# Retention stage written out step by step: side work laid out anew, q's row scale moved into the clip bounds, four buffers of absolute values

## The chip, the core and the metric

The kernel runs on one core of a Trainium2 chip. TensorE (PE) multiplies matrices and writes PSUM, VectorE (DVE) and ScalarE (ACT) work elementwise and read both PSUM and SBUF, GpSimd (POOL) works elementwise on SBUF, and SyncE (SP) issues the DMAs. Each engine takes its own instructions in order; semaphores order the engines among each other. The metric is the device time of one execution in microseconds (us): 2624.17 before, the median of 3 runs (2622.93 to 2625.43).

## The reference, cut to what matters

Eight batches of 1024 tokens (32x32) with 256 channels go through three parts one after the other: a retention layer (with a group norm ahead of it and a residual behind it), a causal attention layer, and a dense mixture of eight experts. The change touches the computation of the first part alone. For every batch and each of 8 heads of 32 channels:

```
q = xf @ Wq.T ; k = xf @ Wk.T * SCALING ; vr = xf @ Wv.T        # xf: group-normed x
qr = theta_shift(q, sin, cos) ; kr = theta_shift(k, sin, cos)   # x * cos + rotate_every_two(x) * sin
qk = einsum('bhqd,bhkd->bhqk', qr, kr) * mask                   # mask[h,i,j] = gamma**dist / sqrt(row sum)
den = clip(abs(qk).sum(-1, keepdims=True), 1.0, 50000.0)
out = einsum('bhqk,bhkd->bhqd', qk / den, vr)                   # then layer norm per head, gelu, @ Wo.T
```

The row sum of the mask factors into a part of the query's row of the image, a part of its column, and head. The kernel applies the decay and the column's part as a window that is multiplied onto the scores; the row's part is one factor for each query row and head.

## The kernel before, in words

The retention layer is `layer0`. A batch has 4 phases p (two groups g of 4 heads, by two halves c of 512 queries), and a phase has 8 steps kt, one for each 128 keys; B = 8 batches make 32 phases and 256 steps. In a step, PE writes the scores of the *next* step for 4 heads (`scores`, L325, two halves j of two heads), then the sums of absolute values of the step before (`sums`, L350, into the PSUM bank `den`), then the weighted values of this step (`weighted`, L339, into `num`). DVE multiplies the scores by the window (`products`, L488, 128x1024, twice a step), and ACT takes their absolute value (`absolutes`, L679, twice a step) into one of four buffers, that is two steps' worth; so it waits until `sums` has read the one of two steps ago (`den_done`, i - 1).

Around these steps lies side work, which each engine has in its own order, by hand, at fixed steps kt. It comes through two more PSUM banks, pA and pB, each a queue of tasks in a fixed order (`A_MID`, `B_MID`); a task on PE first waits (`a_free`, `b_free`) until its predecessor in the bank has been read out.

- Preparation of the next q and k tile: `project` (L264) into pA; the tile is read into t1, for q by DVE with the row scale (`q_rotate_in`, L464), for k by ACT (`k_take`, L659); then `shuffle` (DVE L472), `rotate_cos` (POOL L766), `rotate_sin` (DVE L477), the sum (`split`, POOL L772), a rounded copy (`high`, ACT L666), the remainder (`low`, POOL L779), and 12 DMAs by SP that stack both into qst or kst (L161). t1, t2, hi and lo are single, so the preparations go one behind the other.
- v: `project_v` (L273), read out by ACT (`v_take`, L670).
- The end of a phase, done in the next one (tag 3' is the last phase of the batch before): ACT takes num and den (L683, L687), PE turns them (`transpose_n` L285 into pB, `transpose_d` L291 into pA), DVE takes head sums, centres, clips den (L496, L501, L510), ACT squares (L692), DVE sums (`variance`, L515), POOL works out and applies the factor (`scale_heads`, L794 to L804, with a power at L801), PE turns back (`transpose_z`, L297), ACT applies gelu (L696), and `out_proj` (L307) and `add_residual` (L557) end it.
- Group norm of the next batch: `statistics`, `aggregate` on DVE, two small matmuls `gn1` and `gn2` into pA (L280), `group_mean`, `group_var`, POOL's `group_rstd` (L789), `normalise` (L551). Here gn1 and gn2 stand at kt 2 and 3 of phase 2, and the k projection of that phase at kt 5 and 6.

Batches 0 and 7 are written out; batches 1 to 6 are one body in a hardware loop on each engine (`Fori`), so there are 5 jumps back. The attention part (`layer1_attention`) and the experts (`layer1_experts`) have the same form: first batch, a loop over 6, last batch.

## Time and profile before

| what | value |
|---|---|
| median of 3 runs | 2624.17 us |
| the profiled execution's own time | 2624.51 us |
| its span in the trace | 2622.4 us |
| granted TensorE clock, mean | 0.984 |
| busy: PE, DVE, ACT, POOL | 96%, 70%, 55%, 20% |
| retention up to 1122 us, attention from there to about 1517, experts to the end | |

The busy shares are means over three parts that differ. TensorE works in all of them; what the others' shares mean depends on what TensorE waits for, and that is read from its own rows. Around the span lie 2.1 us that the time of the run has and the trace hasn't.

### The profile page before, as it was taken

Reading aid. Unit: us, or ns where it says so; the run is one execution under the profiler, and the core shown is the slowest. Engines: PE = TensorE matmul, PEld = TensorE weight load, DVE = VectorE, ACT = ScalarE, POOL = GpSimd, SP = SyncE. Lnnn points to the kernel's source line nnn. Section 1 sums busy time; section 2 is a strip of 40 time slices with the busy share of each in tenths; the row PEclk is TensorE's granted clock in tenths of the full one; section 3 lists DMA queues with packets and bytes.
Section 4 is the critical chain, followed back from the end, with each engine's and each line's share of the span. In section 5 each row is a group of like instructions: output and inputs, shape, how many; then the busy total and the mean of one; then the engine's idle time right before and its main releaser. Section 6 shows DMA issues by size and latency. Waiting matters only on the chain. (4 is left out here: it accounts for less than half of the span.)

```text
span 2622.4 us, 43895 instructions
## 1 busy us (share of the span) xinstructions
PE 2512.7 (96%) x15328; PEld 1786.7 (68%) x15328; DVE 1834.2 (70%) x2847; ACT 1449.9 (55%) x2044; POOL 517.6 (20%) x444
## 2 busy tenths in 40 slices
PE   5999999999999999979999969999999999999999
PEld 2444444444444444369999958888888888888888
DVE  4878777777777777657777757666666666666665
ACT  2666565566566566636566545555555555555554
POOL 2333333333333333201212110000000000000000
PEclk8999999999999999989999979999999999999999
DMA  6232222222232222123223143000000000000000
GB/s 233 51 85 60 77 62 79 65 72 75 56 85 59 83 59 70 49 71 111 82 77 115 49 146 106 18 24 24 18 23 24 24 24 24 24 24 24 24 17 16
DMA packets 116786, 157.95 MB, mean 60 GB/s; under 512 B 16272, under 2 KB 82328, under 8 KB 116384
## 3 DMA queue, kind: packets, MB, share of 16 engines
q1 hardware_dynamic: 116640, 156.01, 20.1%
q8 instruction: 91, 1.49, 0.3%
q14 instruction: 55, 0.45, 0.1%
HBM read 72.03 MB, written 33.59 MB: 40 GB/s over the span
## 5 line engine op out<-in xcount | busy, mean ns | idle before, releaser
L488 DVE TENSOR_TENSOR l_prod<-l_scores,l_window 128x1024 f32<-128x1024 f32 x512 | 615.6, 1218 | 220.7 <-PE l_scores L325 186.0
L679 ACT ACTIVATE l_absp<-l_prod 128x1024 f32<-128x1024 f32 x512 | 521.9, 1053 | 282.8 <-PE l_den L350 233.6
L1696 ACT ACTIVATE e_r<-e_h,e_bn,e_rs 128x512 f32<-128x512 f32 x512 | 399.4, 781 | 485.7 <-PE e_h L1547 484.5
L325 PE MATMUL l_scores<-l_qst,l_kst 96*128 96x512 f32 x1024 | 369.3, 457 | 27.9 <-DMA l_qst<-l_lo 12.0
L325 PEld LDWEIGHTS l_scores<-l_qst,l_kst 96*128 96x128 f32 x1024 | 167.4, 190 | 288.3 <-issue 147.9
L1547 PE MATMUL e_y<-e_whi,e_h2lo 128*128 128x256 f32 x1024 | 289.8, 283 | 0.0
L1546 PE MATMUL e_y<-e_wlo,e_h2hi 128*128 128x256 f32 x1024 | 289.7, 283 | 0.0
L1545 PE MATMUL e_y<-e_whi,e_h2hi 128*128 128x256 f32 x1024 | 289.2, 282 | 0.1
L350 PE MATMUL l_den<-l_absp,l_ones 128*32 128x512 f32 x2048 | 274.7, 609 | 0.0
L339 PE MATMUL l_num<-l_prod,l_v 128*32 128x512 f32 x2048 | 269.3, 598 | 0.0
L1791 DVE CAST e_h1hi<-e_r 128x512 fp32r<-128x512 f32 x256 | 111.2, 434 | 224.3 <-ACT e_r L1696 220.2
L1862 POOL TENSOR_TENSOR e_res<-e_res,e_bias 128x1024 f32<-128x1024 f32 x16 | 41.4, 2590 | 930.8 <-DMA e_res<-t_scratch 930.8
L1807 DVE TENSOR_TENSOR e_h2lo<-e_r,e_h2hi 128x512 fp32r<-128x512 f32 x256 | 202.3, 804 | 8.3
L1545 PE MATMUL e_h<-e_xhi,e_whi 128*128 128x512 f32 x512 | 203.0, 397 | 5.0 <-DVE e_wlo L1735 5.0
L1546 PE MATMUL e_h<-e_xlo,e_whi 128*128 128x512 f32 x512 | 202.7, 396 | 0.0
L1547 PE MATMUL e_h<-e_xhi,e_wlo 128*128 128x512 f32 x512 | 200.9, 392 | 0.0
L1545 PEld LDWEIGHTS e_y<-e_whi,e_h2hi 128*128 128x128 f32 x1024 | 196.0, 191 | 5.3 <-DVE e_h2lo L1807 0.3
L1546 PEld LDWEIGHTS e_y<-e_wlo,e_h2hi 128*128 128x128 f32 x1024 | 196.0, 191 | 5.0
L1546 PE MATMUL e_h<-e_h1lo,e_whi 128*128 128x512 f32 x512 | 199.2, 389 | 0.0
L1545 PE MATMUL e_h<-e_h1hi,e_whi 128*128 128x512 f32 x512 | 199.2, 389 | 0.0
L1547 PE MATMUL e_h<-e_h1hi,e_wlo 128*128 128x512 f32 x512 | 199.2, 389 | 0.0
L1547 PEld LDWEIGHTS e_y<-e_whi,e_h2lo 128*128 128x128 f32 x1024 | 196.1, 191 | 0.0
(191 smaller groups left out, 4472.2 us busy)
## 6 DMA issues: line engine op xcount, KB each, us to landing
l_kst<-l_hi SPq DMA_DIRECT2D x256, 64.0 KB, 2.0
l_qst<-l_hi SPq DMA_DIRECT2D x256, 64.0 KB, 2.0
l_raw<-in_xT SPq DMA_DIRECT2D x8, 1024.0 KB, 5.6
l_kst<-l_lo SPq DMA_DIRECT2D x128, 64.0 KB, 2.0
l_qst<-l_lo SPq DMA_DIRECT2D x128, 64.0 KB, 2.0
l_xo<-in_x SPq DMA_DIRECT2D x32, 256.0 KB, 2.8
x_scratch<-l_xo SPq DMA_DIRECT2D x32, 256.0 KB, 2.3
l_xr<-x_scratch SPq DMA_DIRECT2D x8, 1024.0 KB, 8.0
```

The source lines that it names most:

```text
L325: mm = nc.tensor.matmul(sc[j][:, s, :], kst[g][0:96, h, 128 * kt:128 * kt + 128], qst[c][0:96, h, :], start=True, stop=True)
L339: mm = nc.tensor.matmul(num[32 * h:32 * h + 32, :], vsb[g][:, kt, 32 * h:32 * h + 32], prod[2 * (i % 2) + h // 2][:, h % 2, :], start=(kt ...
L350: mm = nc.tensor.matmul(den[32 * h:32 * h + 32, :], ones[:], absp[2 * (i % 2) + h // 2][:, h % 2, :], start=(kt == 0), stop=(kt == KT - 1))
L488: nc.vector.tensor_tensor(prod[n % 4][:], sc[j][:], win[:, 4 * g + 2 * j:4 * g + 2 * j + 2, w0:w0 + QC], ALU.mult).then_inc(prod_ready, 1)
L679: nc.scalar.activation(absp[n % 4][:], prod[n % 4][:], ACT.Abs).then_inc(abs_ready, 1)
L1545: nc.tensor.matmul(o, a[0], b[0], start=start, stop=False, skip_group_check=True)
L1546: nc.tensor.matmul(o, a[0], b[1], start=False, stop=False, skip_group_check=True)
L1547: return nc.tensor.matmul(o, a[1], b[0], start=False, stop=stop, skip_group_check=True)
L1696: nc.scalar.activation(r[m][:], p[m][:], ACT.Relu, bias=bn_[layer][1][:, m, e:e + 1], scale=rs[layer][:, m, e:e + 1]).then_inc(done, 1)
L1791: nc.vector.tensor_copy(h1hi[u % 2][:, m, :], r1[m][:]).then_inc(hi1_ready, 1)
L1807: nc.vector.tensor_tensor(h2lo[u % 2][:, m, :], r2[m][:], h2hi[u % 2][:, m, :].bitcast(F32), ALU.subtract).then_inc(lo2_ready, 1)
L1862: nc.gpsimd.tensor_tensor(flat(res[c][:]), flat(res[c][:]), flat(bias[c][:]), ALU.add).then_inc(biased[c], 1)
```

## The change

In `layer0` the loops over batches go: one Python loop over 256 steps S (phase P = S // 8, kt = S % 8) writes out all instructions of every engine. The side work gets new steps, the same in each phase: on PE q's projection at kt 0, transpose_n at 1, k's projection at 2, transpose_d at 3, output projection at 4 (a second one at 5 where p = 2), v's projection at 6, transpose_z at 7; gn1 and gn2 move from phase 2 to kt 4 and 5 of phase 1, and `normalise` to kt 1 of phase 2. DVE, ACT and POOL are laid out to go with it. The output projection of a batch's first half (o0), which stood at kt 7 of its phase 3, now stands in phase 0 of the next batch, and for the last batch behind the steps.

ACT reads q's projection as it reads k's (`take`), without the row scale; den is clipped against two tables instead of two constants (`clip_den`, two small DVE operations): 1/scale and 50000/scale for each query and head, which gives the same quotient. The absolute values have four steps' worth of buffers (eight tiles of 128x1024, ABS = 4), so ACT waits for the sums of four steps ago. The host makes the tables, and the program reserves less SBUF for DMA scratch. In the attention and expert parts, each `Fori` becomes a Python loop; nothing else changes there.

```diff
-    STEPS, PHASES = 4 * KT, 4
+    PHASES = 4 * B
+    ABS = 4
...
+    def outs(P):
+
+        b = P // 4 - 1
+        if b < 0:
+            return []
+        return {0: [(b, 0, 0)], 1: [(b, 0, 1)], 2: [(b, 1, 0), (b, 1, 1)], 3: []}[P % 4]
...
+    a_tasks = ["gn1", "gn2", "k", "v", "q", "v'", "k'"]
+    b_tasks = []
+    for P in range(PHASES):
+        a_tasks += [("q", P)] if has_q(P) else []
+        a_tasks += [("k", P)] if has_kv(P) else []
+        a_tasks += [("dT", P - 1)] if P else []
+        a_tasks += [("gn1", P), ("gn2", P)] if has_gn(P) else []
+        a_tasks += [("v", P)] if has_kv(P) else []
+        b_tasks += [("nT", P - 1)] if P else []
+        b_tasks += [("o", *o) for o in outs(P)]
+        b_tasks += [("zT", P - 1)] if P else []
+    a_tasks += [("dT", PHASES - 1)]
+    b_tasks += [("nT", PHASES - 1), ("o", B - 1, 0, 0), ("o", B - 1, 0, 1), ("zT", PHASES - 1), ("o", B - 1, 1, 0),
+                ("o", B - 1, 1, 1)]
+    a_order = {t: n for n, t in enumerate(a_tasks)}
+    b_order = {t: n for n, t in enumerate(b_tasks)}
+    o_order = {t[1:]: n for n, t in enumerate(t for t in b_tasks if t[0] == "o")}
...
-        rsc = sb("rowscale", [128, 2, ROWS])
+        bounds = sb("clip", [128, 2, 4, 16])
...
-        absp = [sb(f"absp{n}", [128, 2, QC]) for n in range(4)]
+        absp = [[sb(f"absp{s}_{j}", [128, 2, QC]) for j in range(2)] for s in range(ABS)]
...
-                        if part == 1 and kt == 1 and post:
-                            A("dT" + tag, transpose_d, ph)
-                        if part == 1 and p == 2 and kt == 2 and not last:
-                            A("gn1", group_sums, mv[:, :, 0], agg_done, b + 2)
...
-                        if p != 2 and kt == 3 and prep_kv:
-                            A(f"k{p}", project, wk, (1 - p // 2), p % 2, part)
-                        if p == 2 and kt == 5 + (1 - part) and prep_kv:
-                            pe.wait_ge(xn_ready, 2 * b + 3 + (1 - part))
-                            A(f"k{p}", project, wk, (1 - p // 2), p % 2, 1 - part)
...
-                        if kt == 7 and p == 3:
-                            Bk("o0", out_proj, 0, 0, 4 * b + 3, part)
...
-            body(0, True, False)
-            with pe.Fori(1, B - 1) as b:
...
+            def side_tasks(P, kt, part):
+
+                b, p = P // 4, P % 4
+                G, half = P // 2 + 1, P % 2
+                if kt == 0 and has_q(P):
+                    if part == 0:
+                        a_free(("q", P))
+                    project(wq, (P + 1) // 2 % 2, (P + 1) % 2, (part,))
+                if kt == 1 and part == 0 and P > 0:
+                    transpose_n(P - 1)
+                if kt == 2 and has_kv(P):
+                    if part == 0:
+                        a_free(("k", P))
+                        pe.wait_ge(xn_ready, 2 * (G // 2) + 2)
+                    project(wk, G % 2, half, (part,))
+                if kt == 3 and part == 1 and P > 0:
+                    transpose_d(P - 1)
+                if kt == 4 and part == 1 and has_gn(P):
+                    a_free(("gn1", P))
+                    group_sums(mv[:, :, 0], agg_done, b + 2)
+                if kt == 4 and outs(P):
+                    out_proj(*outs(P)[0], (part,))
+                if kt == 5 and part == 0 and has_gn(P):
+                    a_free(("gn2", P))
+                    group_sums(gvar[:], gvar_ready, b + 2)
+                if kt == 5 and len(outs(P)) == 2:
+                    out_proj(*outs(P)[1], (part,))
+                if kt == 6 and has_kv(P):
+                    if part == 0:
+                        a_free(("v", P))
+                    project_v(G % 2, half, (part,))
+                if kt == 7 and part == 0 and P > 0:
+                    transpose_z(P - 1)
+
+            for S in range(KT * PHASES):
+                for part in range(2):
+                    if S + 1 < KT * PHASES:
+                        scores(S + 1, part)
+                    side_tasks(S // KT, S % KT, part)
+                if S > 0:
+                    sums(S - 1)
+                weighted(S)
+            sums(KT * PHASES - 1)
+            last = PHASES - 1
+            transpose_n(last)
+            transpose_d(last)
+            out_proj(B - 1, 0, 0, (0, 1))
+            out_proj(B - 1, 0, 1, (0, 1))
+            transpose_z(last)
+            out_proj(B - 1, 1, 0, (0, 1))
+            out_proj(B - 1, 1, 1, (0, 1))
...
-            def q_rotate_in(n, a, g, c):
-
-                if not isinstance(n, int) or n > 0:
-                    dve.wait_ge(lo_ready, n)
-                dve.wait_ge(a_ready, a + 1)
-                nc.vector.tensor_tensor(t1[:].rearrange("p (a b) -> p a b", b=32), pA[:].rearrange("p (a b) -> p a b", b=32),
-                                        rsc[:, g, CROWS * c:CROWS * c + CROWS].unsqueeze(2).to_broadcast([128, CROWS, 32]),
-                                        ALU.mult).then_inc(t1_ready, 1)
...
+            def clip_den(P):
+
+                dve.wait_ge(a_ready, a_order["dT", P] + 1)
+                nc.vector.tensor_tensor(dent[:], nT_A[:, :, 0], bounds[:, 0, P % 4, :], ALU.max).then_inc(den_floor, 1)
+                dve.wait_ge(den_floor, P + 1)
+                nc.vector.tensor_tensor(dent[:], dent[:], bounds[:, 1, P % 4, :], ALU.min).then_inc(den_ready, 1)
...
+            for S in range(KT * PHASES):
+                P, kt = S // KT, S % KT
+                b, p = P // 4, P % 4
+                stats_next = b + 1 < B
+                if S == 2 * KT:
+                    dve.wait_ge(window_in, 16)
+                products(S, 0)
+                if kt == 2 and has_q(P):
+                    rotate_sin(prep_q(P), (P + 1) % 2)
+                if kt == 3 and P > 0:
+                    centre(P - 1)
+                if kt == 4 and has_kv(P):
+                    rotate_sin(prep_k(P), P % 2)
+                products(S, 1)
+                if kt == 0 and p == 1 and stats_next:
+                    statistics(b + 1, (2,))
+                if kt == 1 and has_q(P):
+                    shuffle(prep_q(P))
+                if kt == 1 and p == 1 and stats_next:
+                    statistics(b + 1, (3,))
+                if kt == 1 and p == 2 and stats_next:
+                    normalise(b + 1)
+                if kt == 2 and P > 0:
+                    head_sums(P - 1)
+                if kt == 2 and p == 1 and stats_next:
+                    aggregate(b + 1)
+                if kt == 3 and has_kv(P):
+                    shuffle(prep_k(P))
+                if kt == 4 and P > 0:
+                    clip_den(P - 1)
+                if kt == 5 and has_gn(P):
+                    group_mean(b + 1, a_order["gn1", P])
+                if kt == 5 and len(outs(P)) == 2:
+                    add_residual(*outs(P)[0])
+                if kt == 5 and P > 0:
+                    variance(P - 1)
+                if kt == 6 and has_gn(P):
+                    group_var(b + 1, a_order["gn2", P])
+                if kt == 6 and outs(P):
+                    add_residual(*outs(P)[-1])
+                if kt == 7 and p == 0 and stats_next:
+                    statistics(b + 1, (0, 1))
+            last = PHASES - 1
+            head_sums(last)
+            centre(last)
+            clip_den(last)
+            add_residual(B - 1, 0, 0)
+            variance(last)
+            add_residual(B - 1, 0, 1)
+            add_residual(B - 1, 1, 0)
+            add_residual(B - 1, 1, 1)
...
-            def absolutes(b, i, first):
-                for j in range(2):
-                    n = 2 * i + j
-                    act.wait_ge(prod_ready, 2 * STEPS * b + n + 1)
-                    if not (first and i < 2):
-                        act.wait_ge(den_done, STEPS * b + i - 1)
-                    nc.scalar.activation(absp[n % 4][:], prod[n % 4][:], ACT.Abs).then_inc(abs_ready, 1)
...
+            def take(n, a, scale):
+                nc.scalar.activation(t1[:], pA[:], ACT.Copy, scale=scale).then_inc(t1_ready, 1)
...
+            def absolute(S, j):
+                act.wait_ge(prod_ready, 2 * S + j + 1)
+                if S >= ABS:
+                    act.wait_ge(den_done, S - ABS + 1)
+                nc.scalar.activation(absp[S % ABS][j][:], prod[2 * (S % 2) + j][:], ACT.Abs).then_inc(abs_ready, 1)
...
+            for S in range(KT * PHASES):
+                P, kt = S // KT, S % KT
+                absolute(S, 0)
+                if kt == 1 and has_q(P):
+                    take(prep_q(P), a_order["q", P], 1.0)
+                if kt == 3 and has_kv(P):
+                    take(prep_k(P), a_order["k", P], SCALING)
+                if kt == 7 and has_kv(P):
+                    v_take(a_order["v", P], (P // 2 + 1) % 2, P % 2)
+                absolute(S, 1)
+                if kt == 0 and P > 0:
+                    take_num(P - 1)
+                if kt == 0 and P > 1:
+                    gelu(P - 2)
+                if kt == 1 and P > 0:
+                    take_den(P - 1)
+                if kt == 2 and has_q(P):
+                    high(prep_q(P), *stacks_before_q(P))
+                if kt == 4 and P > 0:
+                    squares(P - 1)
+                if kt == 5 and has_kv(P):
+                    high(prep_k(P), *stacks_before_k(P))
+            last = PHASES - 1
+            take_num(last)
+            gelu(last - 1)
+            take_den(last)
+            squares(last)
+            gelu(last)
...
+            for P in range(PHASES):
+                if has_q(P):
+                    rotate_cos(prep_q(P), (P + 1) % 2)
+                    rotated(prep_q(P))
+                    low(prep_q(P), *stacks_before_q(P))
+                if has_kv(P):
+                    rotate_cos(prep_k(P), P % 2)
+                if has_kv(P):
+                    rotated(prep_k(P))
+                if P > 0:
+                    scale_heads(P - 1)
+                if has_gn(P):
+                    group_rstd(P // 4 + 1)
+                if has_kv(P):
+                    low(prep_k(P), *stacks_before_k(P))
+            scale_heads(PHASES - 1)
...
             body(0, True, False)
-            with pe.Fori(1, B - 1) as b:
+            for b in range(1, B - 1):
                 body(b, False, False)
...
-    rowscale = np.stack([factor[4 * g + np.arange(128) // 32] for g in range(2)], 1)
+    tok, t, head = np.arange(128)[:, None, None], np.arange(4)[None, :, None], np.arange(4)[None, None, :]
+    scale = np.stack([factor[4 * (p // 2) + head, (512 * (p % 2) + 128 * t + tok) // R].reshape(128, 16) for p in range(4)], 1)
+    clip = np.stack([1.0 / scale, 50000.0 / scale], 1)
...
-    nc = bacc.Bacc("TRN2", target_bir_lowering=False, num_devices=1)
+    nc = bacc.Bacc("TRN2", target_bir_lowering=False, num_devices=1, dynamic_dma_scratch_size=1024)
```

On PE, the place of the two group-norm matmuls. Before, in phase 2 of batch 0, from the two transposes on (l_bankA is pA, l_bankB is pB):

```order
L285 MATMUL l_bankB<-l_ident,l_tA 128x128 x4
L325 MATMUL l_scores<-l_qst,l_kst 128x512 x2
L291 MATMUL l_bankA<-l_ident,l_tB 128x128 x4
L350 MATMUL l_den<-l_absp,l_ones 32x512 x4
L339 MATMUL l_num<-l_prod,l_v 32x512 x4
L325 MATMUL l_scores<-l_qst,l_kst 128x512 x4
L280 MATMUL l_bankA<-l_mv,l_avg 128x2
L350 MATMUL l_den<-l_absp,l_ones 32x512 x4
L339 MATMUL l_num<-l_prod,l_v 32x512 x4
L325 MATMUL l_scores<-l_qst,l_kst 128x512 x4
L280 MATMUL l_bankA<-l_gvar,l_avg 128x2
```

Now, in phase 1 of batch 0, from transpose_d on:

```order
L290 MATMUL l_bankA<-l_ident,l_tB 128x128 x4
L349 MATMUL l_den<-l_absp_0,l_ones 32x512 x2
L349 MATMUL l_den<-l_absp_1,l_ones 32x512 x2
L338 MATMUL l_num<-l_prod,l_v 32x512 x4
L325 MATMUL l_scores<-l_qst,l_kst 128x512 x4
L277 MATMUL l_bankA<-l_mv,l_avg 128x2
L349 MATMUL l_den<-l_absp_0,l_ones 32x512 x2
L349 MATMUL l_den<-l_absp_1,l_ones 32x512 x2
L338 MATMUL l_num<-l_prod,l_v 32x512 x4
L325 MATMUL l_scores<-l_qst,l_kst 128x512 x2
L277 MATMUL l_bankA<-l_gvar,l_avg 128x2
```

In both, one step lies between transpose_d and gn1; before, transpose_d shared its step with transpose_n. On DVE, what stands between transpose_d's reader and the first matmul's reader has moved. Before, from rotate_sin of q on (phase 2 of batch 0):

```order
L477 TENSOR_TENSOR l_t<-l_t,l_sin 128x512
L488 TENSOR_TENSOR l_prod<-l_scores,l_window 128x1024
L510 TENSOR_SCALAR l_den_t<-l_bankA 128x16
L496 TENSOR_REDUCE l_nsum<-l_bankB 128x16
L488 TENSOR_TENSOR l_prod<-l_scores,l_window 128x1024
L501 SCALAR_TENSOR_TENSOR l_tA<-l_nsum,l_bankB 128x512
L535 COPY l_gmean<-l_bankA 128x2
```

Now, any middle phase, from rotate_sin of q to the clip:

```order
L433 TENSOR_TENSOR l_t<-l_t,l_sin 128x512
L443 TENSOR_TENSOR l_prod<-l_scores,l_window 128x1024
L451 TENSOR_REDUCE l_nsum<-l_bankB 128x16
L443 TENSOR_TENSOR l_prod<-l_scores,l_window 128x1024
L456 SCALAR_TENSOR_TENSOR l_tA<-l_nsum,l_bankB 128x512
L443 TENSOR_TENSOR l_prod<-l_scores,l_window 128x1024
L428 STREAM_SHUFFLE l_t<-l_t 128x512
L443 TENSOR_TENSOR l_prod<-l_scores,l_window 128x1024
L433 TENSOR_TENSOR l_t<-l_t,l_sin 128x512
L443 TENSOR_TENSOR l_prod<-l_scores,l_window 128x1024
L465 TENSOR_TENSOR l_den_t<-l_bankA,l_clip 128x16
L467 TENSOR_TENSOR l_den_t<-l_den_t,l_clip 128x16
```

The head sums, the centring, k's shuffle and k's sine now stand within five products, one between each two, and the clip comes behind them.

## Rows read from the trace of the kernel before

**Rows 1.** Windows: stretch, busy us of PE, PEld, DVE, ACT, POOL, clock, DMA, GB/s.

```profile
54.11:1103.14 1049.03, 1018.46 (x6425) 467.54 (x6428) 808.01 (x961) 646.77 (x753) 383.63 (x344) 0.99 0.26 69
...
1559.00:1800.00 241.00, 241.00 (x1387) 213.27 (x1387) 171.17 (x258) 131.09 (x189) 12.97 (x5) 1.00 0.18 57
1800.00:2480.00 680.00, 680.00 (x3909) 601.57 (x3908) 449.10 (x682) 348.25 (x489) 26.04 (x10) 1.00 0.07 23
```

**Rows 2.** Waits of PE, whole run: total us, times, longest.

```profile
PE l_scores L325 <- issue: 11.6, 5, 2.7
...
PE l_bankA L280 <- DVE l_den_t L510: 8.0, 7, 1.2
...
PE l_bankA L291 <- DVE l_t L464: 7.3, 7, 1.1
...
PE l_scores L325 <- DVE l_prod L488: 3.0, 9, 0.6
...
PE l_scores L325 <- DMA l_kst<-l_lo: 1.0, 1, 1.0
```

**Rows 3.** Timeline, a phase 0 of the loop: start, us, what.

```profile
342.04 0.74 PE L325 MATMUL l_scores<-l_qst,l_kst 96*128 96x512 f32 x2
...
346.74 0.73 PE L325 MATMUL l_scores<-l_qst,l_kst 96*128 96x512 f32 x2
...
350.60 1.21 PE L325 MATMUL l_scores<-l_qst,l_kst 96*128 96x512 f32 x4
...
371.21 1.21 PE L325 MATMUL l_scores<-l_qst,l_kst 96*128 96x512 f32 x4
372.15 2.36 DVE L488 TENSOR_TENSOR l_prod<-l_scores,l_window 128x1024 f32<-128x1024 f32 x2 [1.33 <-PE l_scores L325]
...
374.20 0.73 PE L325 MATMUL l_scores<-l_qst,l_kst 96*128 96x512 f32 x2
```

**Rows 4.** Timeline, PE at a jump back (third batch to fourth).

```profile
440.08 1.06 PE L350 MATMUL l_den<-l_absp,l_ones 128*32 128x512 f32 x8
...
444.62 0.73 PE L325 MATMUL l_scores<-l_qst,l_kst 96*128 96x512 f32 x2 [2.61 <-issue]
...
447.46 1.06 PE L350 MATMUL l_den<-l_absp,l_ones 128*32 128x512 f32 x8
```

**Rows 5.** Timeline, PE around gn1 and gn2, phase 2 of the third batch.

```profile
380.92 1.06 PE L350 MATMUL l_den<-l_absp,l_ones 128*32 128x512 f32 x8
...
385.45 1.79 PE L350 MATMUL l_den<-l_absp,l_ones 128*32 128x512 f32 x8
...
390.19 1.06 PE L350 MATMUL l_den<-l_absp,l_ones 128*32 128x512 f32 x8
```

**Rows 6.** Windows, four us of the same place (columns as in rows 1).

```profile
385.00:389.00 4.00, 3.86 (x19) 1.01 (x19) 2.89 (x8) 1.71 (x2) 0.06 (x1) 0.58 0.00 0
```

**Rows 7.** Timeline, PE before and behind transpose_d, phase 3 of that batch.

```profile
411.37 1.06 PE L350 MATMUL l_den<-l_absp,l_ones 128*32 128x512 f32 x8
...
416.50 1.06 PE L350 MATMUL l_den<-l_absp,l_ones 128*32 128x512 f32 x8
```

**Rows 8.** Lines by form, 66 to 1130 us: busy, mean ns.

```profile
L488 DVE TENSOR_TENSOR l_prod<-l_scores,l_window 128x1024 f32<-128x1024 f32 x500 | 601.2, 1218 | 208.2 <-PE l_scores L325 173.6 <-ACT l_absp L679 31.0
L679 ACT ACTIVATE l_absp<-l_prod 128x1024 f32<-128x1024 f32 x501 | 510.5, 1053 | 271.7 <-PE l_den L350 227.9 <-DVE l_prod L488 42.7
...
L477 DVE TENSOR_TENSOR l_t<-l_t,l_sin 128x512 f32<-128x512 f32 x60 | 54.3, 904 | 0.0
...
L496 DVE TENSOR_REDUCE l_nsum<-l_bankB 128x16 f32<-128x512 f32 x32 | 21.8, 680 | 2.6 <-PE l_bankB L285 2.6
```

**Rows 9.** DMA queue of instructions, 54 to 1104: packets, MB, share.

```profile
q8 instruction: 64, 1.05, 0.5%
```

**Rows 10.** The same, 1560 to 1800 us; from 1800 to 2480 there is none.

```profile
q8 instruction: 12, 0.20, 0.3%
```

**Rows 11.** Waits of PE, behind the last step.

```profile
PE l_bankB L297 <- POOL l_tA L804: 4.0, 1, 4.0
```

613 lines of the change are left out of this document (188 added, 425 removed).

## Prediction, on record before the changed kernel ran

> **What bounds the kernel now.** I read the windows first, since the shares of the page mix three parts. In the retention stretch PE is busy 1018.5 of 1049.0 us, in two stretches of the expert part all of 241 and all of 680 us [rows 1]. So TensorE bounds everything, and the change takes no matmul away. What it can win is time in which PE stands in the retention part. The list of PE's waits says who makes it stand: its own issue 5 times, a reader of pA 7 and 7 times, the products 9 times [rows 2]. These are few places, the same in each batch, so the timeline can price each one. I take the distance from one step's first PE row to the next one's, because the busy time of a matmul is modelled and its start is not.
>
> A step without side work lasts 374.20 - 371.21 = 2.99 us, one with q's projection 346.74 - 342.04 = 4.70, one with two sets of transposes 350.60 - 346.74 = 3.86, so one set is 0.44; a whole phase without a stall is 374.20 - 342.04 = 32.16 us [rows 3]. DVE starts the first product 0.94 us behind the step's first PE row (372.15 - 371.21), two of them take 2 x 1.22, and the next start is at 3.93: in a plain step DVE has 0.57 us to spare [rows 3, 8]. In a phase it has 16 products (19.5), two sines (1.8), two shuffles (I take them as sines, 1.8), four operations of the head-sum kind (2.7), and group norm's share (some 1.5): 27 of 32 us. ACT has 16 absolutes of 1.05 (16.8) and about ten takes and copies of half the width, which I take at 0.6: 23 us [rows 8]. Neither becomes the bound by its sum; each can do so at a place.
>
> **What goes.**
> 1. The jumps back. At one of them PE's step lasts 447.46 - 440.08 = 7.38 instead of 4.70, that is 2.68, of which 2.61 is a wait for issue [rows 4]. The five read in this way are 4.03, 2.68, 2.75, 2.18 and 1.96, together 13.6 us; 11.6 are the waits [rows 2], the first of them has a clock drop besides.
> 2. gn1's wait. The step with gn1 lasts 385.45 - 380.92 = 4.53 [rows 5] and a plain one 2.99. Of the difference of 1.54 I leave some 0.13 for the small matmul itself (an estimate), so 1.4 goes, in 7 batches 9.8 us. In the new order the first reader of transpose_d's bank, the clip, has no head sums ahead of it, and gn1 comes behind it by a whole part of the step.
> 3. The clock behind it. In three batches the step that follows lasts 390.19 - 385.45 = 4.74 [rows 5] instead of 3.1, a plain one with a small matmul; the granted clock of these four us is 0.58, so most of it ran at the lower level, 1.2 GHz, right behind the wait [rows 6]. 3 x 1.64 = 4.9 us. If PE no longer stands there, this goes too.
> 4. transpose_d's wait for `q_rotate_in`. The step lasts 416.50 - 411.37 = 5.13 instead of 3.86, 1.27 more [rows 7], some 1.0 of it the wait [rows 2]; 7 times, 8.9 us. DVE's read of pA waited for POOL's remainder of the k tile; now ACT reads, k's remainder is made in the phase before, and transpose_d comes two steps later.
> 5. The k projection of phase 2 behind `normalise`: 3.0 us of waits for products in all [rows 2], with the restarts 3.6.
>
> Together 40.8 us. The rest of PE's retention time is the same matmuls.
>
> **What comes.** I lay a middle phase out from PE's kt 0 at T = 0: steps start at 0, 4.70, 8.1, 12.8, 16.3, 21.0 (p = 0, 1), 24.0, 28.8 and 32.2. PE needs product j = 0 of a step at that step's start, and j = 1 some 0.57 later, plus half a side task if one stands in between.
> - kt 1: ACT reads q at 3.5 to 4.1, DVE shuffles to 4.9, the next product comes at 5.65: free. den is taken until 5.75 and needed at 6.3: free by half a us, the thinnest place on ACT, since gelu of two phases back now stands ahead of it.
> - kt 2: product at 5.65, sine to 7.8, product to 9.0, needed at 9.6. Head sums to 9.65.
> - kt 3: product to 10.9, centring to 11.5, product to 12.75, needed at 13.4. k is read at 12.05 (after q's remainder, 12.0), shuffled until 13.6.
> - kt 4: product 13.8 to 15.0, sine to 15.9, product to 17.1. PE needs it at 17.7 where an output projection stands in between. In phase 3 there is none, and it is needed at 16.85: a stall of 0.3.
> - kt 5 to 7: clip, variance and one residual fit into 21.0, 24.0 and 28.8 with over 0.5 to spare; POOL has the factor at 25.1, transpose_z wants it at 29.3.
> - Phase 2 has `normalise` (two passes, about 1.6) at kt 1, so kt 2's second product ends at 9.9, needed at 9.6: a stall of 0.35.
> - q's 12 DMAs have landed at about 20.2 and k's copy is made at 21; k's have landed at 31 and q's next copy comes at 42. Nothing queued on SP behind them (a store, a load of x) is due before that.
>
> New stalls: (0.3 + 0.35) x 7 = 4.6 us. Bounds for this term: 0, if the sines run shorter; and 31 phases x 0.7 = 22, if three of the margins of about 0.6 are each missed by 0.2 to 0.3.
>
> DVE gives up one pass of 128x512 (as the head sums, 0.68) a phase, and gains a small second clip; ACT gains 0.6. That lies under PE's 32 us, so nothing for it. The ring of four steps lets ACT run without the sums' pace (227.9 us of its idle time ended with them [rows 8]); PE waited for an absolute nowhere in its list, so by itself nothing: it buys the room for take, gelu and den at kt 0 and 1.
>
> The end. The last o0 leaves the steps (-1.7) and lies in the 4.0 us in which PE waits for POOL [rows 11]. But gelu of phase 30 now stands ahead of `take_den`, and a residual that waits for o0 ahead of `variance`, on the path to POOL's power: I walk it to 2.5 us later. Net +0.8; bounds -3.5 (two projections there run at the lower clock now, and may not) to +3.
>
> The other ten jumps back (attention and experts) cost nothing now: PE has no wait for issue but the five of L325 [rows 2], and its 680 us of experts are full [rows 1]. Retention fetches 64 blocks of instructions in its 1050 us [rows 9], loops included; in the loop stretch of the experts there is none [rows 10]. So the retention body doesn't stay with the engine and the others do. Gain there 0, bounds 0 to 0.3 us.
>
> The Trainium skill, page Runtime: NRT & Kernel Launch, section Instruction fetch mechanics, states that a taken branch with its target outside the current window forces a fetch of the target before execution goes on, and gives that as a reason to unroll. For the retention loop the trace agrees (2.61 us for such a jump [rows 4]). Read as holding for each loop, it would add the ten other jumps; that is the third rival below.
>
> Sum: -13.6 - 9.8 - 4.9 - 8.9 - 3.6 + 4.6 + 0.8 = -35.4. To this I add 2 us for batch 0: PE waits there 1.0 for stacked k [rows 2], which comes a projection later in the new order, and I allow 1 more for small ones: -37.4. Against the profiled execution's 2624.5 (span 2622.4 and 2.1 around it) this gives 2587.1; its time is 0.3 over the median, within the runs' spread. I say 2587.
>
> **The rivals.**
> - *The layout stalls more than walked.* DVE carries two sines, head sums, centring, a shuffle and the clip within kt 2 to 5, some 4.6 us, between ten products. For: the margins are 0.5 to 0.7. Against: the operations are all priced by the same trace, and the steps with projections give back 1.7 us. With the upper bound of 22 instead of 4.6 the time is 2604.
> - *Slower: the instruction stream.* Written out, the loop stretches of attention and experts need blocks that they don't fetch now: at 12 per 240 us [rows 10] 34 in the experts' 680 us, and in attention, at the same pace a us or a faster one, some 15. If each cost PE a stop like a jump back (2.6), that is 127 us: 2587 + 127 = 2714. It decides from 37/49 = 0.75 us a block. Against: in the written-out 241 us the 12 blocks cost nothing that PE shows [rows 1, 10], and 64 in the retention left only 5 waits for issue.
> - *All loops give.* Ten more jumps at 2.6: 2561. Against: rows 1 and 2.
> - *The layout gives nothing.* The stalls at gn1 and transpose_d come back elsewhere (gn2 behind four small DVE operations at kt 5, v behind `group_var` at kt 6, margins 0.8 and 0.1), only the jumps go: 2624.5 - 13.6 + some 3 = 2614.
>
> **How the numbers follow.** Forecast 0.69, more stalls 0.14, nothing but the jumps 0.08, all loops 0.03, slower by the stream 0.04, no change by some mix 0.02. The likeliest one's own range, from the ends of the new stalls and of the tail, is 2578 to 2597. The range to 8 in 10 takes in most of the second case: 2577 to 2602. Faster by over 0.2% (5 us, about what runs that spread by 2.5 us can tell) 0.94, within it 0.02, slower 0.04.
>
> **What would show it.** PE's wait for issue gone from L325; no wait on L277 or L290 above 0.3; no lower clock between the first steps and the last; steps of 2.99 and 4.70 and middle phases of 32.2 to 32.6; PE's busy share of the retention stretch at 0.99; attention and experts as long as before, with instruction blocks all through and no wait for issue. I am wrong if PE waits for products in each phase by over 0.5, if a step lasts longer with no wait named, or if the expert part changes its length.

## The result and the profile after

The changed kernel takes 2586.08 us (median of 4 runs, 2585.49 to 2587.44) against 2623.55 us (4 runs, 2622.75 to 2625.43) of the kernel before: ratio 0.986, 95% interval 0.9845 to 0.9876. The forecast was 2587.0 with a range of 2577 to 2602. The profiled execution has 2585.89 us as its own time and 2584.1 as its span, 38.3 less than the span before.

Where the 38.3 us are, by the starts of PE's rows. The retention stretch runs from the first sums matmul of step 0 to the one of step 254.

| stretch | before | after | difference |
|---|---|---|---|
| up to step 0's sums | 50.76 | 52.35 | +1.6 |
| retention, batch 0 | 127.71 | 125.45 | -2.3 |
| retention, batches 1 to 6 together | 811.53 | 776.60 | -34.9 |
| retention, batch 7 up to step 254 | 111.40 | 111.64 | +0.2 |
| from there to the last output projection | 17.11 | 19.21 | +2.1 |
| on to the end of the experts | | | -5.0 |

The last line is made of small terms of -1.0, -0.9, -1.6, -1.7 and +0.2: the step into attention, attention itself, the step into the experts (there PE waits 6.1 us for the DMA of `e_br`, and 7.7 before), the experts' start, and the rest. I forecast none of them, and they can't be put down to the change: the same wait is 6.1 us in the trace with q read by ACT, which has the loops and the layout of before, and 7.7 in one with the retention's loops written out.

Windows of the changed kernel, with the columns of [rows 1]: the retention stretch, the experts' stretch of 241 us and the one of 680.

```profile
52.35:1066.05 1013.70, 1009.43 (x6423) 465.57 (x6422) 804.97 (x963) 676.26 (x783) 383.75 (x345) 1.00 0.27 72
...
1559.00:1800.00 241.00, 241.00 (x1388) 213.36 (x1387) 161.28 (x246) 124.77 (x177) 12.89 (x5) 1.00 0.09 30
...
1800.00:2480.00 680.00, 680.00 (x3920) 602.32 (x3920) 449.82 (x682) 348.05 (x489) 28.38 (x11) 1.00 0.08 25
```

PE stood for 30.6 us of the retention stretch before (1049.03 - 1018.46) and stands for 4.3 now, and the clock is at its upper level, 2.4 GHz, throughout. PE's waits of the changed kernel (total us, times, longest), those that answer to [rows 2] and [rows 11]; none of them names issue, transpose_d (L290 now) or a gn1 of the six middle batches:

```profile
PE l_bankA L277 <- DVE l_mv L487: 9.1, 1, 9.1
...
PE l_scores L325 <- DVE l_prod L443: 3.4, 4, 1.2
PE l_bankB L297 <- POOL l_tA L707: 3.2, 1, 3.2
...
PE l_bankA L277 <- DVE l_gvar L498: 0.8, 1, 0.8
PE e_y L1456 <- ACT e_wbc L1570: 0.7, 1, 0.7
PE l_bankB L283 <- ACT l_z L623: 0.5, 1, 0.5
```

The two waits of L277 come once each, before the first batch. The four for products lie in batch 0; three of them, 0.5, 1.2 and 1.1 us, are new. The blocks of instructions from 1800 to 2480 us, where there were none before [rows 10]:

```profile
q8 instruction: 31, 0.51, 0.3%
```

The steps of the changed kernel in the middle of its fourth batch (PE's timeline). A step with k's projection, one with transpose_d, one with gn1:

```profile
468.83 1.06 PE L349 MATMUL l_den<-l_absp,l_ones 128*32 128x512 f32 x8
...
473.52 1.06 PE L349 MATMUL l_den<-l_absp,l_ones 128*32 128x512 f32 x8
...
476.94 1.07 PE L349 MATMUL l_den<-l_absp,l_ones 128*32 128x512 f32 x8
...
480.72 0.28 PE L277 MATMUL l_bankA<-l_mv,l_avg 128*128 128x2 f32 x2
...
481.90 1.06 PE L349 MATMUL l_den<-l_absp,l_ones 128*32 128x512 f32 x8
```

They last 4.69, 3.42 and 4.96 us. 3.42 is a plain step and one set of transposes (2.99 + 0.44 by [rows 3]), so transpose_d waits for nothing; with gn1 a step is 0.26 longer than 4.70, where it was 1.54 longer than its plain one [rows 5]. All six middle batches last 129.44 us within 0.02, while before they went from 136.5 down to 132.1.

### The profile page after: what moved, and what is told of

It reads as the page before. It is cut to its first block and busy times, and to the rows that moved or that the text cites. A ratio compares the mean times of both kernels' runs of the same rounds, so it can differ in the third digit from the quotient of the medians.

```text
span 2584.1 us, 40264 instructions
## 1 busy us (share of the span) xinstructions
PE 2503.6 (97%) x15328; PEld 1785.8 (69%) x15328; DVE 1824.4 (71%) x2847; ACT 1479.5 (57%) x2076; POOL 516.8 (20%) x444
## 5 line engine op out<-in xcount | busy, mean ns | idle before, releaser
L605 ACT ACTIVATE l_absp<-l_prod 128x1024 f32<-128x1024 f32 x512 | 540.8, 1056 | 331.4 <-DVE l_prod L443 319.5
L325 PE MATMUL l_scores<-l_qst,l_kst 96*128 96x512 f32 x1024 | 376.3, 459 | 14.6 <-DMA l_qst<-l_lo 9.9
```

The source lines that it names most:

```text
L325: mm = nc.tensor.matmul(sc[j][:, s, :], kst[g][0:96, h, 128 * kt:128 * kt + 128], qst[c][0:96, h, :], start=True, stop=True)
L605: nc.scalar.activation(absp[S % ABS][j][:], prod[2 * (S % 2) + j][:], ACT.Abs).then_inc(abs_ready, 1)
```

## The experiments

Each row is a median with the interval of its ratio to the kernel before as timed beside it, whose median was 2623.4, 2622.1 or 2621.2 us. "Mid batch" is the length of a middle batch of retention by PE's steps.

| kernel | us (runs) | ratio, 95% | mid batch |
|---|---|---|---|
| retention's loops written out | 2635.66 (4) | 1.0031 to 1.0069 | 131.7 |
| the same, 32 small matmuls ahead | 2602.33 (6) | 0.9914 to 0.994 | 131.7 |
| all loops written out | 2599.38 (4) | 0.99 to 0.9936 | 131.7 |
| the same, ring of four | 2599.94 (5) | 0.9902 to 0.9931 | 131.7 |
| den taken earlier | 2620.32 (10) | 0.9975 to 0.9997 | 132 to 136 |
| q read by ACT | 2625.87 (10) | 1.0001 to 1.0021 | 134 to 136 |
| changed, loops in attention and experts | 2588.15 (4) | 0.9847 to 0.9884 | 129.4 |
| the same, 32 small matmuls ahead | 2590.39 (4) | 0.9863 to 0.9899 | 129.4 |
| changed, ring of two | 2633.98 (5) | 1.0025 to 1.0055 | 135.2 |
| changed, one more DVE operation a phase | 2589.09 (4) | 0.9856 to 0.9891 | 129.4 |
| changed, normalise split | 2583.62 (5) | 0.9836 to 0.9865 | 129.04 |
| the same, and the tail reordered | 2581.10 (5) | 0.9831 to 0.986 | 129.04 |

### The loops of retention alone

```diff
-            with pe.Fori(1, B - 1) as b:
+            for b in range(1, B - 1):
```

The same on all five engines, in `layer0` only.

> The kernel before with the retention loops alone written out, nothing moved. My step 1 (the jumps back cost 13.6 us, one clock drop included): 2623.6 - 13.6 = 2610, the five waits for issue on L325 gone, the stalls at gn1 (8.0 us of waits) and at transpose_d (7.3 us) as before. Rival (the written-out stream costs something, or the engines meet the same stall a little later): 2618 or more.

Measured: 2635.66 us, slower than before by 12, so my 2610 was missed. Retention did gain: its stretch went from 1050.64 to 1028.86 us, with no wait for issue and no low clock in it. The loss is in the experts, whose code was not touched. PE's waits of this kernel:

```profile
PE e_h L1545 <- issue: 23.4, 5, 5.0
...
PE l_bankA L291 <- DVE l_t L464: 6.7, 7, 1.0
PE l_bankA L280 <- DVE l_den_t L510: 6.6, 7, 0.9
```

The experts' loop jumps back five times, and each jump now stops PE for up to 5.0 us. Its window from 1791 to 1799 us, around the first of them, and the blocks of instructions from 1760 to 2440 us:

```profile
1791.00:1799.00 8.00, 4.05 (x10) 3.19 (x11) 0.11 (x1) 0.78 (x1) 0.00 (x0) 0.62 0.02 4
```

```profile
q8 instruction: 44, 0.72, 0.5%
```

The granted clock of 0.62 in this window is largely the lower level, 1.2 GHz, right behind the stop. Between two of these jumps, from 1800 to 1940 us, 9 blocks are fetched. Before, this loop fetched nothing [rows 10], and PE was full [rows 1]. So the jump back of a loop is free as long as its code is still held, and something outside the loop decides whether it is.

### The same, shifted by half a block

```diff
+            for _ in range(32):
+                nc.tensor.matmul(pA[0:32, 0:2], ones[:], ones[:, 0:2], start=True, stop=True)
             pe.wait_ge(weights_in, 16 * NWEIGHTS)
```

> The kernel before with the retention loops alone written out (2635.66 in an earlier run: slower than before, as the experts' loop shows five waits for instructions and a lowered clock behind them), and 32 small matmuls more at the very start, while TensorE waits for its weights: some 128 instructions, half of one 16 KB block, whose result nobody uses. Nothing else is changed. Written out, the experts' code takes about 6.5 blocks an iteration (one block each 21.7 us of 140 us), so that it touches 7 or 8 blocks by where it begins. Theory A (whether the experts' loop stays held is decided by where its code lies against the blocks): half a block further it is held again, no issue wait in the experts, and the time is 2603 to 2608. Theory B (the length of the code ahead decides, or the loop of retention had left something that held it): the waits stay, 2635.

Measured: 2602.33 us. With 32 matmuls more the kernel is 33 us faster (32 by the ratios). The experts' window is full again, and their queue of instructions shows one block instead of 44. The two views of this kernel, 1760 to 2440 us:

```profile
1760.00:2440.00 680.00, 680.00 (x3909) 601.61 (x3908) 449.88 (x684) 348.19 (x489) 28.42 (x10) 1.00 0.08 24
```

```profile
q8 instruction: 1, 0.02, 0.0%
```

The code ahead became longer, so it is not its length that hurts, and theory B falls. The shift is about half a block: the trace has 64 matmuls for the 32, and as many weight loads, and the changed kernel has 2 x 15328 of these instructions in 122 blocks of 16.4 KB (2.00 MB), some 250 a block. So the place of the loop's code decides. That it decides by the borders of the blocks (theory A) is a reading that fits the counts and is not shown: straight on, the experts need 31 blocks in 680 us, so 6.4 for one body of 140 us, which by its place touches 7 or 8, and with the stops 9 come in for each body. A single shift was tried here. The Trainium skill, page Runtime: NRT & Kernel Launch, section Instruction fetch mechanics, gives TensorE a store of 128 KiB for instructions and blocks of 16 KiB, which would be eight blocks; the row with one block in 680 us agrees in that such a body can stay, but no run here shows the store's size. The sentence of that section by which a jump out of a window of two blocks forces a fetch does not hold for this loop, whose body is 6.4 blocks long: PE is busy 680.00 of 680.00 us over its jumps.

The reading by blocks throws a doubt on the retention loop. Written out, its code needs 49 blocks in 1000 us (the kernel with all loops written out, 60 to 1060 us), so 6.5 for a body of 131.7 us, hardly more than the experts' 6.4; as a loop it fetched 9 from 307 to 444 us, between two of its jumps. So its stops too may have come from where it happened to lie, and the kernel before with its loops kept and only a shift ahead was not run.

### All loops written out, and then the ring

```diff
-        absp = [sb(f"absp{n}", [128, 2, QC]) for n in range(4)]
+        absp = [sb(f"absp{n}", [128, 2, QC]) for n in range(8)]
...
-                        act.wait_ge(den_done, STEPS * b + i - 1)
+                        act.wait_ge(den_done, STEPS * b + i - 3)
```

The first kernel writes out the loops of all three parts; the second adds this edit, with the indices and the reserved DMA scratch to go with it. The order of the work is that of before in both.

> The kernel before with the loops of all three parts (retention, attention, experts) written out and not one instruction moved. With the retention's loops alone written out the time rose by about 12 us: retention gained about 19 us, and the experts' loop, which in the kernel before had shown no wait for instructions, showed five (up to 5.0 us each) and a lowered clock behind them. Theory A (what cost there was a jump back to code that is no longer held in the chip, and no price lies on code that runs straight on): no jump is left, so the issue waits and the lowered clock of the experts go, retention keeps its 19 us, and the time is 2603 to 2606. Theory B (a long instruction stream costs by its length): the experts run slower still, as all their blocks are fetched, and the time is 2635 or more. Theory C (the experts' loss came with something else of that run): about 2623.

> The kernel before with all loops written out (2599.4 in an earlier run) and its ring of abs tiles made four steps long, the order of the work left as it was. With two tiles the changed kernel took 2634.0 instead of 2586.1, so the ring carries the new layout. Theory A (the ring has its worth only with the new layout, as that puts evictions between ScalarE's abs operations, which must run ahead to make room for them): 2599, within 1.5 us. Theory B (the ring is worth something in the old layout too, where TensorE waits for VectorE's products and for the late evictions): part of the 13.3 us that are left to the changed kernel come with the ring alone, 2588 to 2596.

Measured: 2599.38 and 2599.94 us. All loops together give 22.7 us (2622.06 of the kernel before, timed beside it, to 2599.38), a little more than theory A's range. The experts need 31 blocks from 1760 to 2440 us and PE is full there, so theory B, the price of a long stream, falls. The ring alone gives nothing. What is left to the changed kernel is 2599.38 - 2586.08 = 13.3 us. By the traces the retention stretch gives 15.7 of it (1029.37 to 1013.69), while the start takes 0.5 and the tail 2.0 back. The largest waits in this stretch of the kernel with all loops written out are these two; that they too add up to 13.3 is chance:

```profile
PE l_bankA L291 <- DVE l_t L464: 6.7, 7, 1.0
PE l_bankA L280 <- DVE l_den_t L510: 6.6, 7, 0.9
```

The clock is at the upper level in this kernel from 60 to 1060 us, though gn1's wait is still there:

```profile
60.00:1060.00 1000.00, 985.15 (x6250) 455.28 (x6249) 791.26 (x941) 627.07 (x734) 376.17 (x338) 1.00 0.27 71
```

### The changed kernel with a ring of two

```diff
-    ABS = 4
+    ABS = 2
```

> The changed kernel with the ring of abs tiles put back from four to two, nothing else. Theory A (as forecast, the ring by itself gives nothing: by the trace ScalarE's abs runs right ahead of VectorE's head sums): 2586, within 1 us. Theory B (the new layout lives from the room that the ring gives: with two tiles ScalarE's abs waits for VectorE's head sums, and its evictions behind it come late): one stall of TensorE of 0.3 to 1 us in each of 31 phases, so 2595 to 2617.

Measured: 2633.98 us, 47.9 more than with four, and more than theory B's upper end. (The sums that free the ring are PE's, not DVE's head sums as I wrote above.) Lines by form of this kernel, 66 to 1100 us: what ended the idle time ahead of ACT's absolutes is mostly the sums again, as in [rows 8]; in the changed kernel (the second fence, 66 to 1066 us) it is the products alone.

```profile
L605 ACT ACTIVATE l_absp<-l_prod 128x1024 f32<-128x1024 f32 x494 | 511.1, 1053 | 390.2 <-PE l_den L349 284.2 <-DVE l_prod L443 105.9
```

```profile
L605 ACT ACTIVATE l_absp<-l_prod 128x1024 f32<-128x1024 f32 x502 | 530.2, 1056 | 324.6 <-DVE l_prod L443 312.8
```

The chain, in the timeline of all engines at a step 1 of the kernel with two:

```profile
485.56 1.06 ACT L605 ACTIVATE l_absp<-l_prod 128x1024 f32<-128x1024 f32 x1 [1.55 <-PE l_den L349]
...
486.53 0.58 ACT L587 ACTIVATE l_t<-l_bankA 128x512 f32<-128x512 f32 x1
...
487.26 0.01 DVE L428 LOAD_MASK_SELECT l_t<-l_t  x1 [2.42 <-ACT l_t L587]
...
487.95 0.58 ACT L613 ACTIVATE l_tB<-l_den 128x512 f32<-128x512 f32 x1
...
488.59 1.06 PE L349 MATMUL l_den<-l_absp,l_ones 128*32 128x512 f32 x8 [0.73 <-ACT l_tB L613]
```

ACT's first absolute waits for the sums of two steps ago. Behind it stands q's eviction, for which DVE's shuffle waits, and with it DVE's next product; and behind the second absolute stands the eviction of den, for which PE waits. PE lists these as 22.1 us in 31 waits for L613 and 17.7 in 20 for products:

```profile
PE l_den L349 <- ACT l_tB L613: 22.1, 31, 0.7
PE l_scores L325 <- DVE l_prod L443: 17.7, 20, 1.4
```

So the new layout with a ring of two is slower than the kernel before. Ring and layout belong together: the ring has no price and no gain without the layout.

### Two parts of the change, each on the kernel before

Den taken earlier: the clip moves from the middle of DVE's step 3, where it stood ahead of the head sums, to the end of step 2.

```diff
+                        take_den(A("dT" + tag))
...
-                    if kt == 2 and post:
-                        take_den(A("dT" + tag))
```

> The kernel before with one DVE operation moved: the clip of den from step 3, ahead of the head sums, to the end of step 2. My steps 2 and 3 (gn1 waits for this operation, 1.4 us in 7 batches, and the lower clock follows from the wait, 3 x 1.6): -9.8 - 4.9, so 2609, no lower clock at gn2. Rival a (the wait goes, the clock drops all the same, from other stalls): 2614. Rival b (gn2 or the products wait instead, the DVE having no less to do): 2620 to 2624.

Measured: 2620.32 us, about 3 less, which is rival b's range. gn1's wait of 8.0 us is gone, but its partner one step on has half of it, 0.6 us in each of seven batches (the eighth wait, 0.8, stands at the start in every kernel):

```profile
PE l_bankA L280 <- DVE l_gvar L541: 5.1, 8, 0.8
```

The kernel before has four stretches of some 3.4 us at the lower clock in its middle batches: one behind the first jump back and three behind gn1, of the third to the fifth batch. Here there are three: the one behind the first jump, and two new ones behind the third and the fourth. Behind gn1 and gn2 there is none. PE's timeline at the first of the new ones, and the window around it (columns as in [rows 1]):

```profile
576.27 0.73 PE L325 MATMUL l_scores<-l_qst,l_kst 96*128 96x512 f32 x2 [1.80 <-issue]
```

```profile
570.00:582.00 12.00, 10.20 (x48) 4.69 (x50) 6.19 (x6) 4.56 (x8) 1.28 (x1) 0.86 0.32 72
```

q read by ACT: the row scale is in the clip's bounds, q's read of pA goes from DVE to ACT, at the old steps.

```diff
-                if kt == 1 and prep_q:
-                    q_rotate_in(nq, A(f"q{p}"), g, c)
+                    if kt == 0 and p < 3:
+                        k_take(prep_order(f"q{p}", b), A(f"q{p}"), 1.0)
```

> The kernel before with the row scale alone: q read by ACT at step 0 (in phase 3 behind k's rounded copy), the scale in two tables for the clip. My step 4 said transpose_d's wait goes since ACT reads q. If the reader is what counts: -8.9, 2615. If the wait comes from the late k tile of phase 2 (its remainder on POOL frees t1 for any reader): the wait on L291 stays, now with ACT as its releaser, and the time is 2622 to 2625, or up to 5 slower since ACT blocks its absolutes meanwhile.

Measured: 2625.87 us, no faster. transpose_d waits nearly as long as before (6.5 instead of 7.3 us), now for ACT, and gn1 waits longer (9.5 instead of 8.0 us):

```profile
PE l_bankA L280 <- DVE l_den_t L512: 9.5, 7, 1.4
...
PE l_bankA L291 <- ACT l_t L657: 6.5, 7, 0.9
```

Whoever reads q, t1 is held by the late k tile of phase 2: DVE stood idle 27.7 us in 8 waits for POOL's remainder ahead of this read before, and ACT stands 12.1 us in 8 now. In the changed kernel the wait is gone; which of its new steps takes it away was not tried alone.

### The changed kernel with its other loops kept

```diff
-            for b in range(1, B - 1):
+            with pe.Fori(1, B - 1) as b:
```

On all engines, in attention and experts; and once more with the 32 matmuls ahead.

> The changed kernel with the hardware loops of the attention and expert parts put back. Mine: these loops cost nothing, 2586 (2585 to 2587). Rival (the 4 us that the parts behind the retention gained in the profiled runs come from writing them out): 2590. The page's rule read for every loop: 2612.

> The changed kernel with the hardware loops of attention and experts put back (2588 in an earlier run, no issue wait), and 32 small matmuls more at the very start, while TensorE waits for its first weights anyway: together about 128 instructions of TensorE, half of one 16 KB block of instructions, so that every later loop lies elsewhere against the blocks. The matmuls' result is used by nobody. Theory A (whether a loop's code stays held depends on where it lies against the blocks): the experts' loop may show issue waits at its jumps back, some 3 to 5 us each with a lowered clock behind them, and the time is 2600 to 2617; it stays at 2588 if this shift happens to be a harmless one. Theory B (position does not matter, the length of the code ahead does): 2588, since the length ahead changes by 8 KB only.

Measured: 2588.15 and 2590.39 us. They are 2 and 4 us over the changed kernel, and all three intervals overlap. In both, PE waits nowhere for issue. The shift was a harmless one, so this pair settles nothing about the place of the code; the pair above did.

### How near is DVE now

```diff
+                if kt == 3 and P > 0:
+                    extra()
```

`extra` is a reduction of 128x512 to 128x16.

> The changed kernel with one more reduction of about 0.68 us on VectorE at step 3 of each of the 31 phases of retention that carry side work, written to a tile that nobody reads. It measures how near VectorE is to being the bound now. Theory A (VectorE has slack in each step but at phase 2, about 0.6 us at steps 3 and 4): the time rises by at most 0.1 to 0.3 us a phase, so by 3 to 9 us, to 2589 to 2595. Theory B (VectorE is the next bound in every phase): it rises by nearly the full 0.68 us times 31 = 21 us, to 2607. Theory C (TensorE sets the time with room to spare): unchanged, 2586.

Measured: 2589.09 us, 2585.86 to 2591.69, which overlaps the changed kernel's runs. By the median alone this could be theory A; but the middle batches last 129.44 us as without it. The added operation in lines by form, 66 to 1066 us:

```profile
L456 DVE TENSOR_REDUCE l_spare<-l_cos 128x16 f32<-128x512 f32 x31 | 20.7, 667 | 0.0
```

These 20.7 us of DVE cost PE nothing in a middle batch. The rise of the median is not in the steps (1.0 us of it is in batch 0), so I read it as no change (theory C).

### What is left, taken away

```diff
+                if kt == 1 and p == 2 and stats_next:
+                    normalise(b + 1, (0,), a_order["q", P])
...
-                    normalise(b + 1)
+                    normalise(b + 1, (1,))
```

The first pass stands ahead of q's shuffle and the second behind it. In the changed kernel both stand behind the shuffle, not ahead of it as I had put on record.

> The changed kernel with VectorE's normalise of the next batch in two passes around q's shuffle, at step 1 of phase 2 (both stood ahead of the shuffle). Theory A (normalise holds up the shuffle, that the projection of k, and this the scores: 0.38 us of TensorE at step 2 of phase 2, in seven batches): 2583.4. Theory B (something else than normalise makes that step late): 2586, no change.

Measured: 2583.62 us. The step with k's projection of phase 2 goes from 5.09 to 4.70 us. PE's rows of the changed kernel, and of this one:

```profile
501.43 1.06 PE L349 MATMUL l_den<-l_absp,l_ones 128*32 128x512 f32 x8
...
506.52 1.07 PE L349 MATMUL l_den<-l_absp,l_ones 128*32 128x512 f32 x8
```

```profile
498.51 1.07 PE L349 MATMUL l_den<-l_absp,l_ones 128*32 128x512 f32 x8
...
503.21 1.06 PE L349 MATMUL l_den<-l_absp,l_ones 128*32 128x512 f32 x8
```

A middle batch is 0.40 shorter (129.44 to 129.04), 2.4 us in six. The intervals of the two kernels' runs overlap, but all six batches show it. So normalise is what made this step late, but theory A has the path wrong: normalise never stood ahead of the shuffle. What it held up is DVE's next product, and it was long since its second pass ran beside POOL's multiply by the cosines (`rotate_cos`, released by the shuffle). The two passes took 2.49 us together; split, each takes 0.80. DVE and POOL in the changed kernel, and then in this one:

```profile
499.59 2.49 DVE L507 TENSOR_SCALAR l_xn<-l_raw,l_gmean,l_grstd 128x1024 f32<-128x1024 f32 x2
499.78 1.75 POOL L675 TENSOR_TENSOR l_t<-l_t,l_cos 128x512 f32<-128x512 f32 x1 [10.00 <-DVE l_t L428]
```

```profile
495.48 0.80 DVE L510 TENSOR_SCALAR l_xn<-l_raw,l_gmean,l_grstd 128x1024 f32<-128x1024 f32 x1
...
496.85 0.80 DVE L510 TENSOR_SCALAR l_xn<-l_raw,l_gmean,l_grstd 128x1024 f32<-128x1024 f32 x1
497.04 1.75 POOL L680 TENSOR_TENSOR l_t<-l_t,l_cos 128x512 f32<-128x512 f32 x1 [10.17 <-DVE l_t L428]
```

The first pass also starts at once behind the product, where DVE waited 0.44 us for q's eviction in the changed kernel.

```diff
+            variance(last)
             add_residual(B - 1, 0, 0)
-            variance(last)
...
+            take_den(last)
             gelu(last - 1)
-            take_den(last)
```

> The changed kernel with normalise in two passes, and behind the last step the variance ahead of the first add of the residual and the eviction of the sums ahead of the gelu of the last phase but one. Theory A (both the step of phase 2 and the tail's order hold TensorE up): 2581 to 2583. Theory B (the tail's waits only move on to the next of its chain): as with normalise alone, 2583.4. Theory C (neither moves anything): 2586.

Measured: 2581.10 us, with four runs at 2580.14 to 2582.24 and the profiled one at 2590.34. POOL's 3.2 us are gone from PE's list, but in the profiled run the tail lasts 22.07 us instead of 19.15, at a granted clock of 0.59 from 1065 to 1090 us. So this version is faster than the kernel before; against the one with normalise alone its gain of 2.5 us is not settled, since the intervals overlap and the one trace points the other way.

## Why the prediction came out, step by step

The time was right (2586.1 for 2587), and that PE's stops in the retention part are what the change wins is borne out. But that the two numbers are so near is in part luck. For the retention stretch the forecast has 38.2 us less: 18.5 for the loops (13.6 and 4.9), 17.7 for the layout (9.8, 8.9 and 3.6, less 4.6) and 2 for batch 0. The traces have 37.0 less: 21.3 when the loops are written out and 15.7 from there to the changed kernel. So the loops were put 2.8 too low and the layout with batch 0 4.0 too high. Outside the stretch, the start and the tail cost 3.7, where I had 0.8, and small terms that I didn't forecast give 5.0 back.

1. *The jumps back, -13.6, and 3. the clock behind gn1, -4.9.* The loops written out take 21.3 us from the retention stretch (1050.64 to 1029.37). That is 13.6 + 4.9 + 2.8; the rest is in the waits, which became shorter all over: gn1's 8.0 to 6.6, transpose_d's 7.3 to 6.7, the products' 3.0 to 2.1. But the lower clock was not gn1's alone. I said it would go if PE no longer stands there; in the kernels with the loops written out PE still stands there (6.6 us), and no lower clock is left. With the clip moved alone gn1 stands nowhere, and there are three drops, each right behind a jump back. So without the jumps gn1's stop brings no drop, and without gn1's stop the jumps bring more than before. Two things stay open. gn1's wait is also shorter in the written-out code, 0.94 us in each batch, where it is 1.18 in the loop. And before, this same 1.18 stood in six batches and the clock fell behind three of them. What decides was not tried further. Nor is it shown that the jumps had to go by writing out: see the doubt on the loop's place above.
2. *gn1's wait, -9.8.* With the clip moved by itself 4.3 of the 8.0 us come back at gn2, as the rival of a layout that gives nothing had it, and the stretch is 4.1 us shorter. In the changed kernel, where gn1 stands at a step with an output projection and gn2 at the next, both waits are gone, and 0.26 + 0.23 us a batch is left of the two. With the loops out gn1's wait was 6.6 us.
4. *transpose_d's wait, -8.9.* It went, but the first reason that I gave is wrong: with ACT as the reader it stays. The k tile of phase 2 was late; that its projection at kt 2 instead of 5 is what helps is my reading, not a run of its own. The size of the wait, with the loops out, is 6.7 us.
5. *k's projection of phase 2 and batch 0.* Batch 0 gave 2.3. The forecast has 4.5 for it, the 2 that I allowed and a seventh of the terms counted in seven batches; the new waits for products there, 2.8 us, were in no term. Of the product waits 2.1 us were left without jumps; I had 3.6.

*New stalls, +4.6.* At kt 2 of phase 2 I had 0.35 and 0.39 was there. But I took normalise's two passes at 1.6 us, and they take 2.49, while the sine is shorter than I walked; that the two numbers agree is chance. The 0.3 at kt 4 of phase 3 did not come: the step lasts 2.99 us. DVE's sine takes 706 ns in the changed kernel where it had 904 [rows 8], so each of the two steps with a sine has 0.2 us more than I walked. Lines by form, 66 to 1066 us:

```profile
L433 DVE TENSOR_TENSOR l_t<-l_t,l_sin 128x512 f32<-128x512 f32 x59 | 41.7, 706 | 0.0
```

The mean hides two kinds. Where POOL's multiply by the cosines is already running when the sine starts, the sine takes 884 to 917 ns, in 61 of 64 before and in 8 of 64 now; where POOL isn't at it, 674 to 684, in none before and in 53 now. (In the three at the start POOL begins just behind it, and it takes 691 to 694.) One of before, and one of the changed kernel:

```profile
502.38 1.29 POOL L766 TENSOR_TENSOR l_t<-l_t,l_cos 128x512 f32<-128x512 f32 x1 [2.91 <-DVE l_t L472]
...
503.31 0.91 DVE L477 TENSOR_TENSOR l_t<-l_t,l_sin 128x512 f32<-128x512 f32 x1
```

```profile
499.78 1.75 POOL L675 TENSOR_TENSOR l_t<-l_t,l_cos 128x512 f32<-128x512 f32 x1 [10.00 <-DVE l_t L428]
...
503.14 0.68 DVE L433 TENSOR_TENSOR l_t<-l_t,l_sin 128x512 f32<-128x512 f32 x1
```

*The ring, nothing by itself.* Right from both sides (2599.94 beside 2599.38). That it "buys the room" was said without a price; it is 47.9 us.

*The tail, +0.8.* It is +2.1 to the last output projection, within the bounds I gave; the start's +1.6 was in no term.

*The other ten loops, nothing.* Right for these two kernels: 2588.15 beside 2586.08 is within what can be told. Wrong as a reason: I read the experts' loop as one that stays held, and it stays only where its code happens to lie well. In another kernel of this family the same loop cost some 33 us by its place, and I bounded this term at 0 to 0.3.

Of the rivals, the slow instruction stream would have begun at 0.75 us a block; 31 blocks in 680 us left PE full. The rival of all loops giving 2561 falls too: these windows were full before and are full now.

## What to carry to other kernels

- A loop's price is read where it jumps, in the waits for issue and the queue of instructions, and it is not a property of the loop alone: any edit ahead of it can move its code against the blocks. Here 32 tiny matmuls were worth 33 us. A shift of the code ahead is a cheap test before a loop is written out for its stops; for the retention loop I did not make it. A change that adds or removes code ahead of a loop needs a second look at the loops behind it.
- Price a stall in the layout where it will stand: taken alone, one move passed half of its wait to the next matmul on the bank, and the other its whole wait to the new reader; and a deeper ring that gives nothing before a new layout can carry the whole of it.
- Where one stop lies near another, ask which of them the lower clock follows, before its cost is put down to one.

## What the runs showed of the hardware that I had not expected

- An experts' loop whose code did not change costs nothing, or five stops of up to 5.0 us with a lower clock behind each, by where its code begins: 2602.33 and 2635.66 us. With the stops 9 blocks of instructions come in for each body, without them none.
- A DVE operation can be much longer beside POOL's 128x512 multiply. The sine (two inputs, 128x512) took 884 to 917 ns when it started while that multiply ran, and 674 to 684 without it; the second pass of normalise took 1.77 us instead of 0.80. A DVE operation that started first kept its time (691 to 694 ns; 0.80 us), and POOL's multiply took 1.75 us beside normalise instead of 1.28. In the kernel with all loops written out, too, the 61 sines that started beside POOL took 889 to 919 ns. The traces show this by when the two ran; no kernel was made to take the pair apart.
